# A cross-attention network: each softmax weight's f32 exponential first, its f16 part as a copy of it

## The reference

```python
x = x + L0_xattn(layernorm(x), ctx)   # 16 heads of 64, LoRA, keys: 508 of the context, 4 apart
x = x + L0_ffn(layernorm(x))          # 8 experts, the best 2 of each row
x = x + L1_xattn(layernorm(x), ctx)   # 8 heads of 64, keys: all 512
x = x + L1_ffn(layernorm(x))          # quantised gate, up, down

s = einsum('bhid,bhjd->bhij', q, k) * 64 ** -0.5
p = softmax(s, axis=-1)
o = einsum('bhij,bhjd->bhid', p, v)
```

## Time and profile before

| | us |
|---|---|
| median of 3 runs | 1094.68 |
| lowest and highest of them | 1086.5, 1097.15 |
| the profiled execution, its own time | 1089.7 |
| its span, first to last instruction | 1087.9 |
| TensorE busy | 883.6 |
| VectorE busy | 773.4 |
| ScalarE busy | 718.2 |
| GpSimd busy | 635.4 |

### The profile page before, as it was taken

One profiled execution on the slowest core, in us unless ns is written; L12 is line 12 of the kernel. 1 busy time (PEld: TensorE's weight loads), 2 busy tenths in 40 slices (PEclk: granted clock), 3 DMA queues, 4 the chain that ended last, 5 costly groups with the idle time before them and its releaser, 6 DMA issues. The chain is left out here.

```text
span 1087.9 us, 23374 instructions
## 1 busy us (share of the span) xinstructions
PE 883.6 (81%) x8744; PEld 638.8 (59%) x8744; DVE 773.4 (71%) x1547; ACT 718.2 (66%) x1183; POOL 635.4 (58%) x574
## 2 busy tenths in 40 slices
PE   4887899999999999996543999968888989973476
PEld 4655676767766777775321655645566757663143
DVE  5758778777877886676667444428888887647797
ACT  3487878788878888884243343335797878952674
POOL 2177766766586667674156566542696767852143
PEclk9999999999999999997665999989798999986699
DMA  9479899899989988996492887782999889983155
GB/s 279 156 134 189 154 150 156 142 185 150 178 144 174 162 151 131 164 167 112 121 311 72 168 163 153 157 266 92 177 172 195 144 158 157 178 142 117 24 111 137
DMA packets 504879, 171.11 MB, mean 157 GB/s; under 512 B 477729, under 2 KB 495329, under 8 KB 504737
## 3 DMA queue, kind: packets, MB, share of 16 engines
q1 hardware_dynamic: 501024, 159.39, 77.1%
q0 software_dynamic: 3744, 10.23, 3.4%
HBM read 38.62 MB, written 12.71 MB: 47 GB/s over the span
## 5 line engine op out<-in xcount | busy, mean ns | idle before, releaser
L477 POOL TENSOR_TENSOR A_PHL<-A_pr,A_PHL 128x508 f16<-128x508 f32 x256 | 295.3, 1159 | 135.3 <-ACT A_pr L754 134.6
L753 ACT ACTIVATE A_PHL<-A_ps,A_negmax 128x508 f16<-128x508 f32 x256 | 179.7, 702 | 17.0 <-DVE A_negmax L1003 14.2
L477 POOL TENSOR_TENSOR C_PHL<-C_pr,C_PHL 128x512 f16<-128x512 f32 x128 | 150.2, 1183 | 58.0 <-ACT C_pr L754 57.5
L754 ACT ACTIVATE A_pr<-A_ps,A_negmax 128x508 f32<-128x508 f32 x256 | 181.6, 709 | 0.0
L1003 DVE TENSOR_REDUCE A_negmax<-A_ps 128x2 f32<-128x1016 f32 x128 | 154.2, 1205 | 0.0
L598 PE MATMUL A_ps<-A_K,A_Q 64*128 64x512 f32 x768 | 124.5, 429 | 12.6 <-ACT A_pr L754 10.5
L616 PE MATMUL A_ps<-A_VH,A_PT 128*128 128x65 bf16 (+1 forms) x1024 | 108.1, 196 | 19.8 <-DMA A_PT<-A_PHL 19.6
L616 PEld LDWEIGHTS A_ps<-A_VH,A_PT 128*128 128x128 f16 (+1 forms) x1024 | 92.9, 97 | 47.9 <-DMA A_PT<-A_PHL 28.9
L617 PE MATMUL A_ps<-A_VL,A_PT 128*128 128x64 f16 (+1 forms) x1024 | 107.1, 193 | 0.0
L618 PE MATMUL A_ps<-A_VH,A_PT 128*128 128x65 bf16 (+1 forms) x1024 | 106.8, 194 | 0.0
L753 ACT ACTIVATE C_PHL<-C_ps,C_negmax 128x512 f16<-128x512 f32 x128 | 88.8, 694 | 15.8 <-DVE C_negmax L1003 15.1
(11 more groups left out here) (344 smaller groups left out, 2517.1 us busy)
## 6 DMA issues: line engine op xcount, KB each, us to landing
A_PT<-A_PHL SPq DMA_TRANSPOSE x256, 3.3
M_raw<-in_L_ffn_w_in SPq DMA_DIRECT2D x4, 1024.0 KB, 7.7
M_raw<-in_L_ffn_w_out SPq DMA_DIRECT2D x4, 1024.0 KB, 9.4
C_yc<-routed_rows SPq DMA_DIRECT2D x8, 512.0 KB, 5.4
ct_split<-A_CT SPq DMA_DIRECT2D x4, 768.0 KB, 4.2
C_CT<-ct_split SPq DMA_DIRECT2D x4, 768.0 KB, 8.5
M_rows<-M_xhl SPq DMA_DIRECT2D x4, 512.0 KB, 8.7
out<-X SPq DMA_DIRECT2D x16, 128.0 KB, 2.0
```

What stands on the lines that cost most here:

```text
L477: pool.tensor_tensor(PHL[:, e % PRING, 1, 0:KEYS], pr[:, e % RING, 0:KEYS], PHL[:, e % PRING, 0, 0:KEYS], ALU.subtract).then_inc(pl_ready. ...
L753: a.activation(PHL[:, e % PRING, 0, 0:KEYS], o, ACT.Exp, bias=nm[:, n % 4, h:h + 1])
L754: a.activation(pr[:, e % RING, 0:KEYS], o, ACT.Exp, bias=nm[:, n % 4, h:h + 1]).then_inc(p_ready.sem, 1)
```

## The change

`weights(n)` makes the two f32 exponentials first, one for each head, and each signals a new semaphore, `s_taken`. Only then does ScalarE make the f16 parts, now as copies of `pr` in SBUF and no longer as exponentials of the PSUM bank; each copy waits for `s_taken` of its own head and signals `p_ready`. `scores(n)` waits on `s_taken` in place of `p_ready`. POOL's subtraction still waits on `p_ready`. Both attentions get this.

```diff
@@ -306,6 +306,7 @@
         pj_free = sem("pj_free", len(jobs))
         s_filled = sem("s_filled", G)
         max_ready = sem("max_ready", G)
+        s_taken = sem("s_taken", 2 * G)
         p_ready = sem("p_ready", 2 * G)
         pl_ready = sem("pl_ready", 2 * G)
         pv_done = sem("pv_done", G)
@@ -591,7 +592,7 @@
                 if qt == 0:
                     wait(pe, pj_free, JOB["k", n // U, c % PAIRS] + 1)
                 if n >= 2:
-                    wait(pe, p_ready, 2 * (n - 1))
+                    wait(pe, s_taken, 2 * (n - 1))
                 for m, (i, j) in enumerate(((0, 0), (0, 1), (1, 0))):
                     for h in range(2):
                         r = slice(h * DH, (h + 1) * DH)
@@ -750,8 +751,10 @@
                     o = ps[:, S_BANK + 2 * (n % 2) + h, 0:KEYS]
                     if e >= RING:
                         wait(a, pl_ready, e - RING + 1)
-                    a.activation(PHL[:, e % PRING, 0, 0:KEYS], o, ACT.Exp, bias=nm[:, n % 4, h:h + 1])
-                    a.activation(pr[:, e % RING, 0:KEYS], o, ACT.Exp, bias=nm[:, n % 4, h:h + 1]).then_inc(p_ready.sem, 1)
+                    a.activation(pr[:, e % RING, 0:KEYS], o, ACT.Exp, bias=nm[:, n % 4, h:h + 1]).then_inc(s_taken.sem, 1)
+                for e in (2 * n, 2 * n + 1):
+                    wait(a, s_taken, e + 1)
+                    copy(PHL[:, e % PRING, 0, 0:KEYS], pr[:, e % RING, 0:KEYS]).then_inc(p_ready.sem, 1)
 
             if ipa:
                 wait(a, down_loaded[0], 16)
```

## The result

| | before | after |
|---|---|---|
| median of 20 runs, us | 1090.78 | 1099.80 |
| lowest to highest, us | 1084.61 to 1097.15 | 1087.06 to 1107.62 |
| ratio of the times, 95% interval | | 1.0056 [1.0031, 1.0080] |
| the profiled execution, us | 1089.7 | 1102.94 |

The change makes the kernel slower by 0.56%, about 6 us. That is inside the 1% that I called no change, and it was forecast at +3.1 us. The ratio leaves out executions that took over 1.5% more than the fastest of their kernel (five of the 20 after, none of before), so the two medians differ by more than it says, 9.0 us. The forecast of 1098 started from a median of three runs that was 3.9 us above that of the twenty; that it lies 2 us from 1099.8 is luck, for the step itself was 3 us short by the ratio and 6 us short by the medians.

A forecast was written before the change was run, and what follows sets the result against it. Both attentions were taken as nearly TensorE's own work, stopped by a few waits. The profiled 1089.7 us less 5.9 gain plus 9.0 loss gave 1092.8, +3.1; on the median 1094.68 that is 1097.8, rounded to 1098, range 1088 to 1105.

The forecast's parts named there:

- What the change does inside a unit: ScalarE and POOL: banks free at T+1.26, copies of 0.63 us at a pitch of 0.50, POOL starting 0.51 us later.
- the estimate of 11.5 us for ScalarE: ScalarE: SBUF latency of 0.03 us on each of 384 copies loses 11.5 of the 27 us saved; sum unchanged.
- The score waits: TensorE's `scores` (L598) waiting for ScalarE's exponentials: under 3 us together, from 22.3.
- The loss term: TensorE's weighings waiting on later `PT`: 15 payments of 0.51 us, 7.7, plus 1.3 for near misses, 9.0 us lost.
- The gain term: TensorE's score waits truly given back by banks freed 1.16 us earlier: 5.9 us over A and C.
- Its half for C, 3.0: Score waits in C: 1.2 us kept from the start and three free later ones of 0.6 each, 3.0 us.
- Its half for A, 2.9: Score waits in A: six of 16 meet no `PT` wait within three steps and give back 2.9 us.
- Waits on `PT`: TensorE's waits for the transposed weights: up from 25.6 us by 6 to 15 us, more in number and not longer.
- TensorE's busy time stays: TensorE in both attentions: its busy time would stay unchanged after the edit.
- The ring: Rival: ScalarE's exponentials wait for `pr` slots held by POOL, at most 13 us, 1108 if nothing else; chance 0.04.
- 1075: Rival, the banks pay out: score waits are the true limit and 20.1 us come back; chance 0.12 for 11 or more.
- 1113: Rival, the late parts decide: all 36 weighings pay 0.51 us, 18.4 us lost, no score wait given back; chance 0.12.

The follow-up runs named there:

- late_only: Changed kernel, but `scores` waits on `p_ready` again, so the banks are held until the second copy; ratio 1.0085 to the kernel before.
- LAG 4: Kernel before with `LAG` 4 in A too, each weighing one step later; ratio 1.0048 to the kernel before. The same edit to the changed kernel: 1.0108.
- hybrid: Changed kernel, but the first head has both exponentials from the bank and only the second head's f16 part is a copy; ratio 1.0020 to the kernel before.
- four slots: Changed kernel with four slots of `pr` in C, three in A as before; ratio 1.0088 to the kernel before.
- pool_late: Kernel before, but POOL's first subtraction waits for both heads' exponentials, low parts 1.15 us later; ratio 1.0196 to the kernel before.
- interleave: Changed kernel in the order f32 exponential, copy, f32 exponential, copy; ratio 0.9988 to the kernel before.

## Why the prediction came out right

The sign of the sum held, and the measured time is inside 1% and inside the range: +3.1 us forecast, +6 measured by the ratio. The forecast was for a small difference between two opposite terms, and the runs show the larger of them and leave the smaller unresolved. Point by point:

- *What the change does inside a unit* held nearly to the last digit: banks at T+1.26 (1.27 here), copies of 0.63 (mean 0.636 and 0.632 in A and C), 0.52 apart where I took 0.50, POOL 0.51 late (T+1.85 medians in A, 1.86 in C, from 1.34). The pitch of 0.52 is 0.03 over that of a copy from a bank (0.49), as in the estimate of 11.5 us for ScalarE. ScalarE is busy for 18.9 us less.
- *The score waits* fell under 3 us, as said.
- *The loss term*, 15 separate payments of 0.51 and some near misses, 9.0 us, measured 9.2 with late_only (5.9 to 12.3), and its rule fits at more than double the dose (21 us, 12.5 to 30). The place was less right: it gave A nearly all of it, 13 payments, and C two. A pays at the large dose (26 us of length), but late_only is 4.2 us longer in C, and LAG 4 took nearly all the waits on `PT` out of A without taking the loss of the change. That the total came out so close owes something to luck.
- *The gain term*, 5.9 us, is the weak step. By the ratios 0 to 3 us came back; the intervals still allow the 5.9. Its half for C, 3.0, has no support in this order: C is as long with early banks as without (224.2 to 224.7 in five executions, 224.0 in late_only). Its half for A, 2.9, rests on "free" score waits, those with no wait on `PT` in the three steps after. A is indeed 2 to 6 us shorter in the changed code than in late_only, but hybrid, with POOL on time, has A's waits on `PT` up by 12 us and no gain, and LAG 4 shows the reverse exchange. A wait that no other wait follows in the trace need not be free: what it hides can be a landing for which TensorE was just late enough.
- *Waits on `PT`* grew by 20.5 us and not by 6 to 15: the moved score waits are in it.
- *TensorE's busy time stays* was wrong. In the first pair it grew by 4.4 us in the two attentions at an unchanged idle time. No term of the sum had the clock. In C that repeats. Why the new order spends more of C at half clock is open. Fewer and longer pauses are not enough of a reason: idle times over 1 us sum to 20.3 us before and 24.7 after in C, those under 1 us to 10.7 and 6.2, but hybrid has 24.0 and 5.4 with only 26.2 us at half clock, less than before.
- *The ring* stalls ScalarE's second exponentials by 8.7 us in A and 5.7 in C, by the same sum, 14 us where I had set 13 as the most, and in C taking it away gained nothing. It was rightly given little.

Both rivals at the ends, 1075 and 1113, are out.

## What to carry to other kernels

When an engine is 92% busy, as TensorE is in A, and stands for two different reasons in turn, the sums of the two waits are no price list. Shorten one and the other grows; here 20 us moved over in the changed kernel, and with LAG 4 14.7 us went the other way for 11.2, and no stage got clearly shorter. Before freeing a buffer early, look at what the same edit makes later, and give that the price: here the transposes, 0.5 us later in each unit, cost more than the banks, 1.16 us earlier, gave. If both can be had with little lateness (exponential, copy, exponential, copy: 0.08 late, banks half a microsecond early), take that order rather than the changed one; here it was level with before, and no variant beat before clearly.

## What the runs showed of the hardware

TensorE's granted clock can fall to half right behind a pause, and matmuls take longer then. In the changed kernel, C, a pause of 2.83 us ends at 908.47, and the granted clock is 0.50, the 1.2 GHz level, from 909 to 912 us and 1.00 again after it. TensorE is busy in all 3 us. The rows, the pause first:

```profile
908.47 0.38 PE L581 MATMUL C_ps<-C_WOh,C_OTh 128*128 128x256 f32 x1 [2.83 <-DVE C_OTl L879]
```

```profile
909.00:912.00 3.00, 3.00 (x18) 2.93 (x17) 1.48 (x2) 0.52 (x2) 2.92 (x3) 0.50 0.25 47
912.00:957.00 45.00, 43.40 (x550) 32.81 (x548) 31.30 (x46) 40.56 (x73) 34.39 (x30) 1.00 0.98 162
```

Over the executions the price can be read off C, where the same matmuls took 187.3 us of busy time with 20.1 us at half clock (LAG 4, before), 190.8 with 30.3 (before) and 195.4 with 42.8 (four slots): an estimate of 0.36 us for each microsecond. Through all fourteen rows of the table it is 0.39, with one of them (pool_late) 1.6 us off the line. Part of the difference between two profiles of the same code is this; A varied by 3 us in that of before and by 4 in the changed.

A ScalarE instruction that waits for the end of the one just before it started 0.13 to 0.16 us later than one that follows freely. From an exponential to its copy it is 0.70 to 0.71 us in interleave and 0.72 in hybrid, where exponentials with satisfied waits are 0.57 apart. First an exponential and its copy in interleave, then two exponentials in hybrid, the second of which waits for nothing:

```profile
303.11 0.67 ACT L754 ACTIVATE A_pr<-A_ps,A_negmax 128x508 f32<-128x508 f32 x1
303.81 0.63 ACT L688 ACTIVATE A_PHL<-A_pr 128x508 f16<-128x508 f32 x1
```

```profile
303.11 0.68 ACT L755 ACTIVATE A_pr<-A_ps,A_negmax 128x508 f32<-128x508 f32 x1
303.67 0.68 ACT L757 ACTIVATE A_PHL<-A_ps,A_negmax 128x508 f16<-128x508 f32 x1
```
